# Grouping the value products of a two-pass attention and splitting its causal mask matmuls over the array's row halves

## Chip, cores and metric

The kernel runs on one core of a Trainium2 chip. The metric is device time in microseconds (us) of one execution. TensorE (PE in the rows) runs matmuls, ScalarE (ACT) the exponentials, VectorE (DVE) the row maxima, GpSimd (POOL) masks and small work, and SyncE (SP) issues most transfers.

## What is computed

The reference has two layers, each an attention and a mixture of experts on x (4 x 256 tokens x 128 features) with a context of 4 x 512 tokens x 64 features:

```python
x = x + tanh(g_xattn[0]) * L0_xattn(layernorm(x), ctx)   # 16 heads of 8: causal self-attention plus cross-attention
x = x + tanh(g_ffn[0])   * L0_ffn(layernorm(x))          # 8 experts, top 2, capacity 160
x = x + tanh(g_xattn[1]) * L1_xattn(layernorm(x), ctx)   # one head of 128
x = x + tanh(g_ffn[1])   * L1_ffn(layernorm(x))          # 8 experts, top 2, dense
...
att = einsum('bhqd,bhkd->bhqk', q, k) * scale
att = where(tril, att, -inf)
y   = einsum('bhqk,bhkd->bhqd', softmax(att), v)         # the same again against the context, and added
```

The change lies in the first layer's attention.

## The kernel before

There are 64 pairs of batch and head. Four heads are a quad, so there are 16 quads, numbered 0 to 15; the code's `n` is a quad and `NG` is 16. Two heads that lie in the upper and the lower 64 rows of the array are a pair (`par` 0 and 1). Both passes below work on a pair at once: two matmuls of 64 rows, one for each half of the array, run side by side.

**Pass one** finds the row maxima of the scores. Its units are listed in `pass1`, 96 in all. A "cross" unit is two matmuls of 512 columns (L1410). A "late" unit covers the second 128 queries of two pairs, an "early" unit the first 128 queries of four pairs; both need the causal mask, which is added in PSUM by multiplying an identity with a mask tile (L1402) before the scores are accumulated on it (L1412, L1415). A late unit has 4 mask matmuls and 4 of scores, an early unit 8 and 8. A "turn" unit transposes the maxima (L1387). Each unit fills two of the banks 0 to 3; VectorE reduces it (L1042), and a unit may start when the unit two before it has been reduced (`s1_free`). For every half batch there are 8 cross, 2 late, 1 early and 1 turn.

**Pass two** has 96 steps, six to a quad (k = 0 to 5). `scores2(step)` computes transposed scores of a pair into two banks of a ring of three (banks 4 to 6), and ScalarE takes the exponential of each (L843) into a slot of probabilities. A step of scores therefore has to wait until only one exponential of the step before is left to do:

```python
place = s2_place[2 * step + 1]
if place >= S2_RING:
    pe.wait_ge(p_in, place - S2_RING + 1)
```

`values(n, r)` is round r (0 to 5) of a quad's value products: the four heads write to four groups of 32 columns of the array, with all 128 rows (L1468). Rounds 0 and 1 are the self-attention (256 and 128 columns), 2 to 5 the context (256 columns each). The products of quad n - 1 are issued in the steps of quad n, as `ROUNDS_AT[k]` says. ScalarE takes the finished sums of an earlier quad from bank 7 into `ot_sb` behind the first exponential of a quad (L818), TensorE transposes them in step k = 1 behind the value products (`turn_values`, L1486), and ScalarE takes the result into `o_sb` (L833).

TensorE's order in a step is written out by hand: the pass-one unit that is due, `scores2(step)`, the rounds of `ROUNDS_AT[k]`, at k = 1 `turn_values`, and in steps 81, 83, 89, 91 and 94 work for the output projection and the router (`route_early`). Eighteen units of pass one stand ahead of step 0, then one unit ahead of each step up to step 78. SyncE lays the maxima into `qcat` for the half batch (L550) behind its other loads, and pass two waits for them at steps 0, 12, 24 and so on.

Of the kernel before, what the change touches and what calls it, by code (L numbers as in the profile page):

```python
# [6 lines left out]
BF16 = mybir.dt.bfloat16  # L7
U32 = mybir.dt.uint32
ALU = mybir.AluOpType
# [3 lines left out]
P = 128  # L13
BANK = 512
EPS = 1e-5
CAPACITY_FACTOR = 1.25
NEG = -1.0e30
# [9 lines left out]
def flamingo_gated_kernel(nc, a, out):  # L27
    B, S, D = a["x"].shape
# [15 lines left out]
    PAIR, PAR = H // 2, 2  # L44
# [14 lines left out]
    with ctx:  # L59
        def sb(name, shape, dt=F32):  # L60
            return ctx.enter_context(nc.sbuf_tensor(name, shape, dt))
# [20 lines left out]
        b_col = sb("b_col", [P, 3])  # L82
        b1_col = sb("b1_col", [P, 1])
        bv_col = sb("bv_col", [P, 1])
        bv_wide = sb("bv_wide", [P, D])
        bp_v = sb("bp_v", [P, D])
        b_p = sb("b_p", [P, D])
        b_g = sb("b_g", [P, E])
# [3 lines left out]
        gw_t = sb("gw_t", [P, 2, E])  # L92

        ident = sb("ident", [P, P])
        ident_b = sb("ident_b", [P, P], BF16)
        mask_b = sb("mask_b", [P, P], BF16)
        upto_b = sb("upto_b", [P, P], BF16)
        ones_b = sb("ones_b", [P, KW], BF16)
        iota_e = sb("iota_e", [P, E])
# [56 lines left out]
        def q_place(first, n):  # L156
            return qcat[:, :].rearrange("p a b n -> p (a b n)").bitcast(F32)[:, first:first + n]
# [45 lines left out]
        AFTER_HH = 2 * NF0 * SLOTS  # L203
        eo = q_place(AFTER_HH, 2 * 3 * D).rearrange("p (s t d) -> p s t d", s=2, t=3)
        got = sb("got", [P, 2, NT, D])
        k1_t = q_place(AFTER_HH + 6 * D, NC * P)
        sg = qk_r[:, :, SC:SC + BANK]
        acc = k_place(3, 0, NT * D).rearrange("p (t d) -> p t d", t=NT)
# [13 lines left out]
        def bank(i, n=1):  # L222
            return psum[:, i * BANK:(i + n) * BANK]
# [89 lines left out]
        def linker(eng, s):  # L313

            count = [0]

            def link(ins):
                count[0] += 1
                ins.then_inc(s, 1)
                eng.wait_ge(s, count[0])  # L320
            return link
# [71 lines left out]
        def groups_of(i):  # L393

            return {0: ((0, 2), (2, 4), (4, 8)), 1: ((0, EARLY), (EARLY, 8))}.get(i, ((0, 4), (4, 8)))
# [55 lines left out]
        NG = NHEAD // QUAD  # L451
        STEPS = 3 * QUAD // 2
        TURN_AT = 1
        ROUNDS_AT = ((), (0, 1), (2,), (3,), (4,), (5,))

        TAIL = NG - 5
        assert pass1_before(STEPS * (TAIL + 2)) == len(pass1)
# [136 lines left out]
        def _(pool):  # L594
            link = linker(pool, pool_step)
            made = [0]

            def const(ins):

                made[0] += 1  # L600
                ins.then_inc(consts, 1)
                pool.wait_ge(consts, made[0])
# [3 lines left out]
                                     fill=1.0, base=0, channel_multiplier=1))  # L606
# [4 lines left out]
            def rstd_group(i, first, end):  # L611

                tiles = slice(first, end)
                pool.wait_ge(stats_in[i], end)
                link(pool.tensor_scalar(ln_rstd[:, tiles], ln_mv[:, tiles, 1], EPS, None, ALU.add))
                pool.tensor_tensor(ln_rstd[:, tiles], ln_rstd[:, tiles], half_neg[:, tiles],
                                   ALU.pow).then_inc(rstd_in[i], 1)
# [7 lines left out]
            const(pool.memset(c_t[DC:DC + 1, SC:NC * P], 1.0))  # L625
            for first, end in groups_of(0)[1:]:
                rstd_group(0, first, end)
            const(pool.tensor_copy(ident_b[:, :], ident[:, :]))
            link(pool.memset(mask_b[:, :], 0.0))
            const(pool.affine_select(out=mask_b[:, :], in_=mask_b[:, :], pattern=[[-1, P]], compare_op=ALU.is_ge,  # L630
                                     fill=NEG, base=0, channel_multiplier=1))
            pool.wait_ge(zero_in, 2)
            const(pool.affine_select(out=upto_b[:, :], in_=ones_b[:, 0:P], pattern=[[1, P]], compare_op=ALU.is_ge,
                                     fill=0.0, base=0, channel_multiplier=-1))
# [62 lines left out]
            for head in range(NHEAD):  # L697
                for n in split_before.get(head, ()):
                    split_max(n)
                if head == 5 * QUAD:  # L700
# [5 lines left out]
                                   base=0, channel_multiplier=-1).then_inc(masked, 1)  # L706
# [22 lines left out]
            for e in range(E):  # L729
                pool.wait_ge(dn_taken[0], e + 1)  # L730
                for t in range(NST):
# [3 lines left out]
                                            in_=eo[0:m, e % 2, t, :], in_offset=None, bounds_check=2 * TOK - 1,  # L735
# [586 lines left out]
        def _(pe):  # L1322
# [54 lines left out]
            def pass1_unit(i):  # L1377
                u = pass1[i]
                if i >= 2:
                    pe.wait_ge(s1_free, i - 1)  # L1380
                first = 2 * (i % 2)
                if u[0] == "turn":
                    pe.wait_ge(split_in, u[1] + 1)
                    for t in range(QT):
                        dst = bank(first)[0:2 * PAR * 3 * PP, t * P // 2:(t + 1) * P // 2].bitcast(BF16)
                        src = nmax_p[:, u[1] % 2, PAR * t:PAR * t + PAR].rearrange("p r c q -> p (r c q)")
                        ins = pe.transpose(dst, src, ident_b[:, :])  # L1387
                    ins.then_inc(s1_full, 1)
                    return
                kind, part, t, g = u  # L1390
                b = part // 2
                if kind == "cross" and t == 0 and g == 0:
                    pe.wait_ge(cat_in[b], 16 * 2 * NPROD)
                    pe.wait_ge(pad_in[b], 16 * 4)
                if kind == "late" and part == 0:
                    pe.wait_ge(self_in, 16 * NPROD)
                heads = {"cross": 1, "late": 2, "early": 4}[kind]
                if kind != "cross":
                    for par in range(PAR):
                        dst, w = bank(first + par), BANK // heads  # L1400
                        for n in range(heads):
                            pe.matmul(dst[:, (n + 1) * w - P:(n + 1) * w], ident_b[:, :], mask_b[:, :],  # L1402
                                      start=(n == 0), stop=False, skip_group_check=True)
                for n in range(heads):
                    for par in range(PAR):
                        half = slice(64 * par, 64 * par + 64)
                        q, k = qcat[half, b, heads * g + n], kcat[half, b, heads * g + n]
                        dst = bank(first + par)
                        if kind == "cross":
                            ins = pe.matmul(dst, q[:, S + t * P:S + (t + 1) * P], k[:, S:KW], start=True, stop=True)  # L1410
                        elif kind == "late":
                            ins = pe.matmul(dst[:, n * S:(n + 1) * S], q[:, P:S], k[:, 0:S], start=False, stop=True,  # L1412
                                            skip_group_check=True)
                        else:
                            ins = pe.matmul(dst[:, n * P:(n + 1) * P], q[:, 0:P], k[:, 0:P], start=False, stop=True,  # L1415
                                            skip_group_check=True)
                ins.then_inc(s1_full, 1)
# [25 lines left out]
            def values(n, r, heads=range(QUAD)):  # L1443

                part = 0 if r < 2 else 1 + (r - 2) // 2
                if r == 0:
                    if n <= TAIL:
                        pe.wait_ge(ot_in, n)
                    else:
                        pe.wait_ge(ot_in, n - 1)  # L1450
                    pe.wait_ge(o_clear, 1 + int(n > TAIL))
                    pe.wait_ge(masked, QUAD * n + heads[-1] + 1)
                if n == NG - 1:
                    pe.wait_ge(p_in, s2_place[unit_of(QUAD * n + heads[-1], part)] + 1)
                elif r == 2:
                    pe.wait_ge(p_in, s2_place[3 * QUAD * (n + 1) - 1] + 1)
                for j in heads:
                    head = QUAD * n + j
                    b, h = head // H, head % H
                    p = p_slots[unit_of(head, part) % NPT]  # L1460
                    if r < 2:
                        p = p[:, (0 if r == 0 else S):(S if r == 0 else S + P)]
                        cols, v = slice(r * P, S), QT * b + r
                    else:
                        c = r - 2
                        p = p[:, (c % 2) * S:(c % 2 + 1) * S]
                        cols, v = slice(S, 2 * S), NT + CT * b + c
                    ins = pe.matmul(bank(o_bank(n))[32 * j:32 * j + HA, cols], v_aug[:, v, h, :], p,  # L1468
                                    start=r in (0, 2), stop=r in (1, ROUNDS - 1), skip_group_check=True)
                if r == ROUNDS - 1 and heads[-1] == QUAD - 1:  # L1470
                    ins.then_inc(pv_done, 1)
# [97 lines left out]
            for step in range(STEPS * NG):  # L1569

                n, k = step // STEPS, step % STEPS
# [4 lines left out]
                if n >= 1:  # L1576
                    for r in ROUNDS_AT[k]:
                        values(n - 1, r)
# [176 lines left out]
            for s in range(NHT):  # L1755
                pe.wait_ge([ht_act, ht_dve][s][2], 1)
                pe.matmul(bank(4 + s), w1_q[:, :], h_t[:, s * BANK:(s + 1) * BANK],
                          start=True, stop=True).then_inc(q1_full, 1)
# [61 lines left out]
```

## Time and profile before

| | |
|---|---|
| median of 3 runs | 378.12 us (374.95 to 379.81) |
| the profiled execution | 374.34 us, of which the span from first to last instruction is 372.6 |
| mean granted TensorE clock | 0.948 |
| busy in the span | TensorE 326.8 us, VectorE 233.9, ScalarE 191.7, GpSimd 110.0 |
| first to last step of pass two | 45.7 to 178.4 us |

A time in a row below is in us from the start of the span. Where several instructions are merged in a row, the second number is the time from the start of the first to the end of the last. The end of a matmul is modelled, so the spacing of the starts tells more of TensorE than the durations.

### The profile page before, as it was taken

The numbers are of one execution on the slowest core, as the hardware profiler recorded it, in microseconds if no ns is written. First come the engines' busy times: TensorE is split into PE (matmuls) and PEld (weight loads), VectorE is DVE, ScalarE is ACT, GpSimd is POOL, SyncE is SP. The second block draws the span as 40 slices with busy tenths as digits, with TensorE's granted clock in tenths as the row PEclk, the third lists the DMA queues.
The fourth block names the chain that finished last, engine by engine and source line by source line (L and its number), as shares of the span: only waits on it lengthen the run. The fifth ranks groups of instructions, "written<-read, shape, count | busy, mean of one in ns | idle before, by whom it ended". The sixth has DMA issues, their size and how long they took to land.

```text
span 372.6 us, 7109 instructions
## 1 busy us (share of the span) xinstructions
PE 326.8 (88%) x2696; PEld 188.9 (51%) x2696; DVE 233.9 (63%) x546; ACT 191.7 (51%) x397; POOL 110.0 (30%) x202
## 2 busy tenths in 40 slices
PE   4689799979999999789989799999987599899994
PEld 2446433424434344244476467677755266565662
DVE  5889998858888879466442143332213679649765
ACT  3267388858898888557248323322247143323220
POOL 5526231316433233123575003443350201100000
PEclk9999879989999999899989699999998599989999
DMA  7759792960323005230161560000004000000001
GB/s 177 172 124 210 132 195 56 213 187 4 115 74 102 4 2 173 73 102 3 26 214 35 128 184 10 18 23 21 10 21 118 0 0 3 0 0 2 28 1 28
DMA packets 35777, 27.80 MB, mean 75 GB/s; under 512 B 5579, under 2 KB 33022, under 8 KB 35744
## 3 DMA queue, kind: packets, MB, share of 16 engines
q1 hardware_dynamic: 33574, 25.27, 27.4%
q0 software_dynamic: 1280, 1.88, 1.6%
q8 instruction: 21, 0.34, 0.4%
q10 hardware_dynamic: 890, 0.20, 0.3%
q14 instruction: 12, 0.10, 0.1%
HBM read 11.89 MB, written 5.26 MB: 46 GB/s over the span
## 4 chain that ended last, share of the span: by engine, by line
PE 69%; DVE 13%; ACT 6%; DMA 4%; issue 4%; POOL 2%; ACTq 1%; SPq 0%; POOLq 0%; DVEq 0%
PE psum L1468 12%; PE psum L1672 11%; PE psum L1703 7%; PE psum L1691 4%; DVE nmax L1042 4%; PE psum L1434 4%; PE psum L1650 4%; PE psum L1410 3%; PE psum L1486 3%; PE psum L1402 3%; ACT ot_sb L818 2%; PE psum L1412 1%; PE psum L1655 1%; PE psum L1765 1%; PE psum L1437 1%
## 5 line engine op out<-in xcount | busy, mean ns | idle before, releaser
L1042 DVE TENSOR_REDUCE nmax<-psum 128x2 f32<-128x1024 f32 (+2 forms) x88 | 103.2, 1216 | 15.6 <-PE psum L1410 11.3
L843 ACT ACTIVATE parts<-psum 128x512 f32<-128x512 f32 (+1 forms) x88 | 44.7, 569 | 9.3 <-PE psum L1434 8.8
L1672 PE MATMUL psum<-p_more,kcat 128*128 128x320 f32 x128 | 42.6, 475 | 0.7 <-DVE p_more L1176 0.7
L1185 DVE TENSOR_TENSOR qcat<-psum,qk_r 128x320 f32<-128x320 f32 x32 | 15.7, 491 | 42.8 <-ACT qk_r L886 42.6
L733 POOL DMA_INDIRECT rows_back<-qcat,back_at x24 | 22.9, 953 | 53.1 <-ACT qcat L876 48.2
L886 ACT ACTIVATE qk_r<-psum 128x320 f32<-128x320 f32 x32 | 14.0, 437 | 45.2 <-PE psum L1672 45.2
L1703 PE MATMUL psum<-h_t,kcat 128*128 128x512 f32 x64 | 30.9, 608 | 0.7 <-ACT h_t L854 0.7
L1410 PE MATMUL psum<-kcat,qcat 64*128 64x512 bf16 x128 | 25.9, 404 | 5.5 <-DVE nmax L1042 4.8
L1672 PEld LDWEIGHTS psum<-p_more,kcat 128*128 128x128 f32 x128 | 23.4, 200 | 13.5 <-issue 4.6
L1468 PE MATMUL psum<-parts,v_aug 128*9 128x256 f32 (+1 forms) x352 | 28.9, 373 | 0.0
L1434 PE MATMUL psum<-qcat,kcat 64*128 64x256 bf16 x256 | 25.6, 280 | 3.0 <-ACT p_more L843 1.2
L1468 PE MATMUL psum<-qk,v_aug 128*9 128x256 f32 (+1 forms) x160 | 26.5, 369 | 0.5
L1468 PE MATMUL psum<-qk_r,v_aug 128*9 128x256 f32 (+1 forms) x160 | 26.5, 369 | 0.0
L900 ACT ACTIVATE qk_r<-psum 128x512 f32<-128x512 f32 x16 | 9.6, 597 | 32.6 <-PE psum L1703 32.6
L843 ACT ACTIVATE qk<-psum 128x512 f32<-128x512 f32 (+1 forms) x40 | 20.5, 563 | 10.5 <-PE psum L1439 7.8
L843 ACT ACTIVATE qk_r<-psum 128x512 f32<-128x512 f32 (+1 forms) x40 | 20.3, 551 | 5.6 <-PE psum L1434 3.5
L1691 PEld LDWEIGHTS psum<-kcat,qcat 128*128 128x128 f32 x128 | 17.4, 202 | 9.0 <-issue 5.8
L866 ACT ACTIVATE kcat<-psum 128x512 f32<-128x512 f32 x24 | 14.1, 597 | 12.5 <-PE psum L1599 11.4
L1410 PEld LDWEIGHTS psum<-kcat,qcat 64*128 64x128 bf16 x128 | 6.3, 94 | 26.8 <-DVE nmax L1042 15.0
L1234 DVE TENSOR_TENSOR qcat<-psum,qk_r 128x512 f32<-128x512 f32 x16 | 11.0, 688 | 14.0 <-ACT qk_r L900 8.3
L713 POOL DMA_INDIRECT rows_in<-h_rows,put_at x16 | 16.0, 1000 | 8.5 <-DVE put_at L1153 4.4
L1691 PE MATMUL psum<-kcat,qcat 128*128 128x128 f32 x128 | 18.1, 288 | 0.5 <-DVE qcat L1234 0.5
(225 smaller groups left out, 609.5 us busy)
## 6 DMA issues: line engine op xcount, KB each, us to landing
kcat<-parts SPq DMA_DIRECT2D x18, 192.0 KB, 4.1
qcat<-parts SPq DMA_DIRECT2D x24, 128.0 KB, 3.9
kcat<-ones_b SPq DMA_DIRECT2D x8, 192.0 KB, 5.2
kcat<-in_L_ffn_wi_gate_dram SPq DMA_DIRECT2D x6, 256.0 KB, 3.8
kcat<-in_L_ffn_wi_up_dram SPq DMA_DIRECT2D x6, 256.0 KB, 4.0
kcat<-in_L_ffn_wo_dram SPq DMA_DIRECT2D x6, 256.0 KB, 5.5
parts<-in_L_ffn_w_dram SPq DMA_DIRECT2D x3, 512.0 KB, 5.5
rows_in<-zeros SPq DMA_DIRECT2D x1, 1290.0 KB, 5.8
```

The costliest lines, as they stand in the source:

```text
L713: pool.indirect_dma_start(out=rows_in[0:E * SLOTS, :], out_offset=bass.IndirectOffsetOnAxis(ap=put_at[:, k, t:t + 1], axis=0), in_=h_rows[ ...
L733: pool.indirect_dma_start(out=rows_back[:, :], out_offset=bass.IndirectOffsetOnAxis(ap=back_at[0:m, e, t:t + 1], axis=0), in_=eo[0:m, e % ...
L843: act.activation(p_slots[u % NPT][:, 0:w], s2_bank(s2_place[u])[:, 0:w], ACT.Exp, scale=SCALE).then_inc(p_in, 1)
L1042: dve.tensor_reduce(dst[:, :, n * g:n * (g + 1)], src.rearrange("p (r q k) -> p r q k", r=PAR, q=n), AX.X, ALU.max, negate=True).then_inc( ...
L1185: dve.tensor_tensor(hh[:, e % 2, f, 0:SLOTS], bank(3 + 2 * (i % 2))[:, 0:SLOTS], sg[:, i % 2, 0:SLOTS], ALU.mult).then_inc(hh_in[0], 1)
L1410: ins = pe.matmul(dst, q[:, S + t * P:S + (t + 1) * P], k[:, S:KW], start=True, stop=True)
L1434: ins = pe.matmul(dst[:, c * S:(c + 1) * S], k[:, key:key + P], q[:, S:QW], start=True, stop=True)
L1468: ins = pe.matmul(bank(o_bank(n))[32 * j:32 * j + HA, cols], v_aug[:, v, h, :], p, start=r in (0, 2), stop=r in (1, ROUNDS - 1), skip_grou ...
L1650: pe.matmul(bank(6)[:, t * D:(t + 1) * D], hh[:, e % 2, f, t * P:(t + 1) * P], w_t[e][:, 2, f * P:(f + 1) * P], start=(f == 0), stop=(f == ...
L1672: ins = pe.matmul(bank(2 + 2 * (i % 2) + m)[:, 0:SLOTS], w_t[e][:, m, f * P:(f + 1) * P], xs_t[:, e % 2, :], start=True, stop=True)
L1691: ins = pe.matmul(bank(DN_BANK[n % 4])[:, t * P:(t + 1) * P], hh1[:, n % 2, t * P:(t + 1) * P], w1_t[:, e, 2, :], start=True, stop=True)
L1703: ins = pe.matmul(bank(2 + 2 * (i % 2) + m), w1_t[:, e, m, :], h_t[:, s * BANK:(s + 1) * BANK], start=True, stop=True)
```

## The change

`ROUNDS_AT` puts rounds 0, 1 and 2 of the value products into step k = 1 and rounds 3, 4 and 5 into step k = 3; steps 2, 4 and 5 have none. The mask of a late or early unit is added in two turns, each with matmuls of 64 rows, alternately for the upper and the lower half of the array and for the two banks; a bank's mask takes one matmul from each half of the mask's rows, so there are twice as many mask matmuls (8 in a late unit, 16 in an early one), of the same 128 columns. For the shifted operands the identity and the mask become 256 columns wide, built by GpSimd at the start with one memset more. `bv_wide` becomes a part of `got`.

```diff
-        bv_wide = sb("bv_wide", [P, D])
...
-        ident_b = sb("ident_b", [P, P], BF16)
-        mask_b = sb("mask_b", [P, P], BF16)
+        ident_w = sb("ident_w", [P, 2 * P], BF16)
+        mask_w = sb("mask_w", [P, 2 * P], BF16)
+        ident_b = ident_w[:, P // 2:P // 2 + P]
...
+        bv_wide = got[:, 0, 0, :]
...
-        ROUNDS_AT = ((), (0, 1), (2,), (3,), (4,), (5,))
+        ROUNDS_AT = ((), (0, 1, 2), (), (3, 4, 5), (), ())
...
+            link(pool.memset(ident_w[:, :], 0.0))
             const(pool.tensor_copy(ident_b[:, :], ident[:, :]))
-            link(pool.memset(mask_b[:, :], 0.0))
-            const(pool.affine_select(out=mask_b[:, :], in_=mask_b[:, :], pattern=[[-1, P]], compare_op=ALU.is_ge,
-                                     fill=NEG, base=0, channel_multiplier=1))
+            link(pool.memset(mask_w[:, :], 0.0))
+            const(pool.affine_select(out=mask_w[:, :], in_=mask_w[:, :], pattern=[[-1, 2 * P]],
+                                     compare_op=ALU.is_ge, fill=NEG, base=P // 2, channel_multiplier=1))
...
-                    for par in range(PAR):
-                        dst, w = bank(first + par), BANK // heads
+                    w = BANK // heads
+                    for turn in range(2):
                         for n in range(heads):
-                            pe.matmul(dst[:, (n + 1) * w - P:(n + 1) * w], ident_b[:, :], mask_b[:, :],
-                                      start=(n == 0), stop=False, skip_group_check=True)
+                            for par in range(PAR):
+                                rows = slice(64 * par, 64 * par + 64)
+                                shift = slice(64 * (1 + par - turn), 64 * (1 + par - turn) + P)
+                                pe.matmul(bank(first + par)[:, (n + 1) * w - P:(n + 1) * w], ident_w[rows, shift],
+                                          mask_w[rows, shift], start=(turn == 0 and n == 0), stop=False,
+                                          skip_group_check=True)
```

## Rows read from the trace of the kernel before

**Rows 1.** The page: shares of the chain that ended last.

```profile
PE 69%; DVE 13%; ACT 6%; DMA 4%; issue 4%; POOL 2%; ACTq 1%; SPq 0%; POOLq 0%; DVEq 0%
```

**Rows 2.** The chain in order of time, ScalarE's taking of sums: start, us, what.

```profile
88.29 0.60 ACT ot_sb L818
...
95.58 0.60 ACT ot_sb L818
...
104.08 0.60 ACT ot_sb L818
```

**Rows 3.** Timeline of quad 5, with a turn and cross units only.

```profile
88.44 0.11 PEld L1434 LDWEIGHTS psum<-qcat,kcat 64*128 64x128 bf16 x4 [0.41 <-ACT p_more L843]
...
90.39 0.29 ACT L833 ACTIVATE o_sb<-psum 128x144 f32<-128x144 f32 x1 [0.15 <-PE psum L1486]
90.51 0.11 PEld L1434 LDWEIGHTS psum<-qcat,kcat 64*128 64x128 bf16 x4
...
90.94 1.91 ACT L843 ACTIVATE parts<-psum 128x512 f32<-128x512 f32 x4 [0.25 <-PE psum L1434]
...
93.06 2.17 ACT L843 ACTIVATE parts<-psum 128x512 f32<-128x512 f32 x4 [0.22 <-PE psum L1434]
...
93.51 0.39 PE L1410 MATMUL psum<-kcat,qcat 64*128 64x512 bf16 x2
...
93.74 0.38 PE L1434 MATMUL psum<-qcat,kcat 64*128 64x256 bf16 x4
94.05 0.39 PE L1468 MATMUL psum<-qk,v_aug 128*9 128x256 f32 x1
```

**Rows 4.** Timeline of TensorE in quad 6, which has the masks.

```profile
100.04 0.40 PE L1402 MATMUL psum<-mask_b,ident_b 128*128 128x128 bf16 x4
100.37 0.39 PE L1412 MATMUL psum<-kcat,qcat 64*128 64x256 bf16 x4
100.59 0.38 PE L1434 MATMUL psum<-qcat,kcat 64*128 64x256 bf16 x4
100.91 0.62 PE L1468 MATMUL psum<-parts,v_aug 128*9 128x256 f32 x8
101.46 0.62 PE L1402 MATMUL psum<-mask_b,ident_b 128*128 128x128 bf16 x8
102.01 0.40 PE L1415 MATMUL psum<-kcat,qcat 64*128 64x128 bf16 x8
102.25 0.38 PE L1434 MATMUL psum<-qcat,kcat 64*128 64x256 bf16 x4
```

**Rows 5.** Busy time of the engines in quads 5 and 6, by windows.

```profile
core 0: us, PE busy (x) PEld busy (x) DVE busy (x) ACT busy (x) POOL busy (x), PEclk, DMA share, GB/s
...
88.30:95.60 7.30, 6.78 (x90) 2.63 (x88) 5.91 (x8) 6.67 (x16) 6.20 (x12) 1.00 0.27 104
95.60:104.00 8.40, 8.24 (x116) 3.73 (x114) 7.44 (x8) 6.60 (x15) 2.52 (x7) 1.00 0.11 40
```

**Rows 6.** Waits of TensorE from 54 to 180 us: total, times, longest.

```profile
PE psum L1437 <- DMA qcat<-nmax_t: 2.4, 1, 2.4
PE psum L1387 <- POOL nmax_p L690: 1.8, 1, 1.8
...
PE psum L1506 <- POOL h_rows L668: 0.8, 1, 0.8
```

**Rows 7.** TensorE alone by windows: length, busy, granted clock, DMA share, GB/s.

```profile
40.80:44.20 3.40, 1.55 (x11) 0.95 0.55 100
44.20:47.60 3.40, 2.58 (x14) 0.50 0.50 139
...
156.80:160.20 3.40, 2.47 (x32) 1.00 0.93 273
```

**Rows 8.** Timeline of TensorE in quad 13, at the low clock.

```profile
153.53 0.61 PE L1434 MATMUL psum<-qcat,kcat 64*128 64x256 bf16 x4 [0.58 <-ACT p_more L843]
...
156.52 0.39 PE L1434 MATMUL psum<-qcat,kcat 64*128 64x256 bf16 x4
```

**Rows 9.** Timeline of GpSimd behind its constants.

```profile
25.97 2.61 POOL L654 TENSOR_TENSOR qk_r<-qk,parts 128x1280 f32<-128x1280 f32 x1 [7.75 <-ACT parts L810]
```

## The prediction

> **What bounds the kernel now.** I read the page's chain first: TensorE carries most of it [rows 1]. That average hides that the stretch the change touches has two limits in turn. So next I took the chain in order of time. The taking of sums by ScalarE (L818) is on it once in every quad, and its starts are a ruler: 7.29 us from 88.29 to 95.58, then 8.50 us to 104.08 [rows 2]; eight starts from 88.29 to 142.97 alternate so. Quads with only cross units and a turn take 7.29, quads with three masked units 8.5. The windows say why [rows 5]: in the short quad ScalarE is busy 6.67 of 7.30 us and in the long one 6.60 of 8.40, while TensorE is busy 8.24 of that 8.40. ScalarE's work is the same; it starves longer where TensorE has masks. So a long quad is TensorE's, a short one ScalarE's but for short gaps.
>
> The timeline of the short quad shows the gaps. At the head of a quad TensorE itself waits for an exponential (0.41 before 88.44). Then it issues scores, rounds 0 and 1 and the transposes; the next scores start only at 90.51, and ScalarE idles 0.15 before taking the turned sums and 0.25 before its next exponential at 90.94 [rows 3]. From there four exponentials in 2.17 us, 0.54 each, follow one another. A step then is 1.09 us, two exponentials, and TensorE fits in exactly.
>
> **What one move costs.** A change of shape on the array costs 0.11 us: a round of 256 columns is eight matmuls on four column groups, 0.44 at the spacing of the tail of a group, and the next group starts after 0.55 (100.91 to 101.46); eight full-array masks of 128 columns are 0.44 and the next group starts after 0.55 again (101.46 to 102.01); early scores to pass-two scores, both 64-row shapes, take 0.24 with nothing added (102.01 to 102.25), late ones 0.22 (100.37 to 100.59) [rows 4]. Pass-two scores are 0.22 (0.31 to the values behind them, 93.74 to 94.05), a cross unit 0.23, and from the start of a step's scores to its exponential 0.43 (90.51 to 90.94) [rows 3].
>
> **Grouping the rounds, as a gain.** Before, value products interrupt the 64-row shapes in five steps of a quad, after in two. Three visits less are six changes of shape, 6 x 0.11 = 0.66 us of TensorE time in each of 15 quads. Nothing of the streaming goes away. In a short quad that time isn't on the path at all.
>
> **Grouping the rounds, as a loss.** The ring of three banks sets ScalarE's cover. Scores of a step may start when the first exponential of the step before is done. ScalarE then has three exponentials left to do, 3 x 0.54 = 1.63, and TensorE notices about 0.06 late, so 1.57. Within that TensorE must issue these scores, the rounds, the next pass-one unit, and get the next scores out. Before: 0.22 + 0.11 + 0.44 + 0.11 + 0.22 + 0.43 = 1.53. It fits, by 0.04, which is what the timeline shows. With three rounds in step 3: 0.22 + 0.11 + 3 x 0.43 + 0.11 + 0.22 + 0.43 = 2.38, which is 0.81 beyond the cover. ScalarE starves 0.81 there. In steps 2, 4 and 5 TensorE gets free early, but can't give it back: the same ring stops it, and ScalarE already runs at its own rate. In step 1, where ScalarE starves 0.15 + 0.25 already, round 2 adds its whole 0.43. A short quad so grows by 0.81 + 0.43 = 1.24 us, to 8.5.
>
> **A long quad.** ScalarE's work of 6.6 to 6.9 us is the same as in a short one, and the starving in step 1 as well (0.4 + 0.43). In the path of step 3 a late unit (0.44) takes the place of a cross unit (0.22), so 0.81 + 0.22 = 1.03. The early unit in step 5 fits: 0.22 + 0.68 + 0.43 = 1.33 against 1.57. The short quad's 7.29 + 0.43 + 1.03 is 8.75, and 0.1 more where a cross unit follows the transposes with a change of shape: 8.85, against 8.50. So a long quad turns from TensorE's to ScalarE's and grows by 0.35. Two quads together: +1.6 us.
>
> **The masks.** Each bank's mask now takes two matmuls of 64 rows. Alternating halves run side by side if they do as the early scores do, eight in 0.24; then the streaming stays 0.22 (late) and 0.44 (early), and one or two changes of shape, 0.11 or 0.22, go in each of 24 masked units. Bounds: 0.22 saved in each, or the halves don't overlap and a late mask costs 0.22, an early one 0.44 more. The nearest row, L1415, is the same shape in the same order with different banks, so I take the first [rows 4]. The gain alone would be 0.33 in a long quad, 2 us over six of them; behind the grouped rounds most of it lies where TensorE waits for ScalarE anyway, and it is in the 8.85. The masked units before step 0 stand between full-array projections, so their number of changes stays. If the halves don't overlap, the late unit in step 3's path adds 0.22 per long quad, and the early unit in step 5 makes that path 0.22 + 0.88 + 0.24 + 0.43 = 1.77, 0.20 beyond the cover: 0.42 in each of six quads, 2.5 us in all. GpSimd's extra memset and the doubled widths lie ahead of 7.75 idle us [rows 9]: nothing. `bv_wide` in `got`: nothing, since `got` is filled in the second half of the span.
>
> **Round 2 earlier, other queues.** Round 2 waits for the last exponential of its quad. By the ring that is done before the scores of step 1 start, so nothing new. The sums of a quad are complete two steps earlier; ScalarE's taking, which waits for them, isn't late now. Behind a delayed step stand VectorE's maxima and GpSimd's masks, both with more room than before, and the expert loads on SyncE, which have the whole of pass two as cover.
>
> **The sum.** Quads 1 to 3 would grow by 1.2 + 0.35 + 1.2 = 2.7, but at step 24 TensorE waits 2.4 us for a transfer of the maxima [rows 6] that SyncE issues at the end of an unbroken series of loads which started before step 9. That wait takes the growth up: +0.3. Quads 4 to 11 are four pairs: 4 x 1.6 = +6.4. Quad 12: +0.35, and behind it the wait of 1.8 for GpSimd's split is passed on. Quads 13 to 15 have no pass one. Step 1 costs 0.43, and step 3's path is 2.38 - 0.22 = 2.16 against 1.57, 0.59: together 1.0 in each, +3.0. Against that, round 5 is gone from the end (-0.4), the wait of 0.8 for `h_rows` in step 81 falls where the delay arrives, and the rounds taken from steps 82, 83 and 94 leave projection and router work to start sooner; I take 1.8 for these two together, between the 0.8 of the row and 0.8 + 3 x 0.43. Sum: 0.3 + 6.4 + 0.35 + 3.0 - 0.4 - 1.8 = 7.85, say **+7.9 us**, +2.1%. The rest of the kernel, expert layers and second attention, is shifted and not changed.
>
> The profiled execution took 374.34 us, 1.7 beyond its span of 372.6; it would become 382.2. The median of the runs lies 3.8 above that execution. So the forecast for a median is 378.1 + 7.9 = **386.0 us**.
>
> **Rival A, TensorE alone decides (faster).** If the exponentials were not the limit, the 0.66 of every quad would come off: 15 x 0.66 = 9.9, and 0.1 to 0.2 of 24 masks, about 3: 378.1 - 13 = 365. For it speaks that TensorE is busy 8.24 of 8.40 us in a long quad. Against it: ScalarE's busy 6.67 of 7.30 in a short one, and the 0.04 us that the cover has to spare. It decides from the point at which three rounds together take no more than 0.44 + 0.04 = 0.48 us, against 1.29 by the rows. A mixture of it and the forecast, where ScalarE overlaps more than I think, lands within 2% on the faster side. The Trainium skill, "TensorEngine Tiling (Array Packing)", Key Properties, says that changing the tiling mode drains the engine; the 0.11 us agrees, and by that rule alone the change would come out as this rival. Chance 0.12.
>
> **Rival B, the clock falls too (slower still).** After the change TensorE waits for ScalarE some 2.8 us in a short quad, instead of 0.9, most of it from step 3's end to the next quad's step 1. In the trace the clock went from 2.4 to 1.2 GHz (granted 0.50) behind a stretch in which TensorE was busy 1.55 of 3.40 us; behind one with 2.47 it stayed up [rows 7]. By the same rows' way of counting, a light stretch after the change has six bursts of about 0.39 in 3.6 us, some 2.3 busy, nearer to the second. If it falls, the price per time is in quad 13: 2.99 us from the scores of step 1 to those of step 2 [rows 8], against 2.07 - 0.23 = 1.84 without the turn unit [rows 3], so 1.15. In seven of the quads: +8, 394 us. The Trainium skill, "TensorE: Matmul & The Clock Gate", A second HAM failure mode, tells of matmul groups with short idle pieces between them that make the clock go down and up; no run here has such a stretch yet. Chance 0.17.
>
> **Rival C, something absorbs it (no change).** The k = 3 stall needs every exponential behind it to be late. If more of the delay falls into waits that stand already (2.4, 1.8 and 0.8 us, [rows 6]), +3 remains: 381. For it: these waits are real. Against it: between steps 24 and 72 there is none. Chance 0.11.
>
> **How the numbers follow.** The forecast has 0.60. Two per cent, 7.6 us, is about what a measurement of this kernel tells from no change, and the forecast's +7.9 stands on that bound: half of its 0.60 on either side, since its terms are good to 2 us or so. Slower 0.30 + 0.17 = 0.47, same 0.30 + 0.11 = 0.41, faster 0.12. The range leaves out A, and takes in C, and B up to its seven quads: 378 to 394.
>
> **What would show it.** Right: starts of L818 8.5 and 8.85 us apart; ScalarE idle about 0.8 to 1.0 before the exponential of step 4, once a quad; TensorE waiting for L843 in steps 3 and 5; a round behind a round spaced 0.44; no wait for the transfer at step 24 or a short one; masks with 0.06 from pair to pair, and no 0.11 behind them. Wrong: L818 under 7.3 us apart in short quads (the ring doesn't hold TensorE as I read it), three rounds in less than 1.2 us, masks at 0.11 a pair, or a granted clock under 1 between 90 and 145 us.

## The result, and the profile after

| | before | after |
|---|---|---|
| median | 378.6 us (4 runs, 374.95 to 379.81) | 386.82 us (4 runs, 383.73 to 388.28) |
| ratio | 1 | 1.0232, 95% interval 1.0185 to 1.0279 |
| profiled execution | 374.34 us | 388.28 us |
| busy TensorE, ScalarE | 326.8, 191.7 us | 325.0, 191.2 us |

The change makes the kernel 8.2 us slower at the medians. Slower is clear of the noise; whether it is by more than 2% the interval leaves open. The forecast was 386.0 us, range 378 to 394. Ratios and intervals here and below are estimated from the fast executions alone and need not equal the quotient of the medians beside them. No engine has more to do: busy TensorE time even falls by 1.8 us. The time is in waiting, and the ruler of [rows 2] finds it first. The chain in order of time, after, ScalarE's taking of sums (L820 now):

```profile
89.90 0.60 ACT ot_sb L820
...
98.45 0.60 ACT ot_sb L820
...
107.23 0.60 ACT ot_sb L820
```

The short quad is 8.55 us, forecast 8.5 (7.29 before); the long one 8.78, forecast 8.85 (8.50 before). Two quads have grown by 1.54, forecast 1.6. The windows of these two quads, after:

```profile
core 0: us, PE busy (x) PEld busy (x) DVE busy (x) ACT busy (x) POOL busy (x), PEclk, DMA share, GB/s
90.20:98.80 8.60, 7.08 (x92) 2.83 (x88) 6.34 (x8) 6.69 (x15) 6.16 (x12) 1.00 0.34 127
98.80:107.50 8.70, 7.86 (x132) 4.10 (x130) 7.06 (x8) 6.57 (x15) 2.59 (x8) 1.00 0.01 2
```

Against [rows 5], ScalarE's 6.69 us now stand in 8.60 instead of 7.30, and TensorE is idle more in both. The granted clock is full. The timeline of the short quad, after, shows the two gaps, one in step 1 and one behind step 3:

```profile
90.06 0.39 PE L1440 MATMUL psum<-qcat,kcat 64*128 64x256 bf16 x4
...
92.44 0.29 ACT L835 ACTIVATE o_sb<-psum 128x144 f32<-128x144 f32 x1 [0.58 <-PE psum L1492]
92.56 0.39 PE L1440 MATMUL psum<-qcat,kcat 64*128 64x256 bf16 x4
...
92.98 1.90 ACT L845 ACTIVATE parts<-psum 128x512 f32<-128x512 f32 x4 [0.25 <-PE psum L1440]
...
93.64 0.28 PE L1443 MATMUL psum<-qcat,kcat 64*128 64x256 bf16 x2 [0.47 <-ACT parts L845]
...
93.90 0.39 PE L1474 MATMUL psum<-qk,v_aug 128*9 128x256 f32 x2
...
95.32 0.39 PE L1416 MATMUL psum<-kcat,qcat 64*128 64x512 bf16 x2
95.55 0.38 PE L1440 MATMUL psum<-qcat,kcat 64*128 64x256 bf16 x4
...
95.96 2.17 ACT L845 ACTIVATE parts<-psum 128x512 f32<-128x512 f32 x4 [1.08 <-PE psum L1440]
96.61 0.39 PE L1440 MATMUL psum<-qcat,kcat 64*128 64x256 bf16 x4 [0.47 <-ACT parts L845]
...
97.69 0.28 PE L1443 MATMUL psum<-qcat,kcat 64*128 64x256 bf16 x2 [0.27 <-ACT parts L845]
```

In [rows 3] ScalarE idled 0.15 before the turned sums; now 0.58, which is round 2's 0.43. Behind the three rounds of step 3 (93.90 to 95.32, that is 1.42 = 3 x 0.43 + 0.11 and a little) ScalarE idles 1.08 before its next exponential; in the row of before at the same place, 93.06, it was 0.22. The growth is 0.86, forecast 0.81. Elsewhere TensorE waits for an exponential before the scores of step 3 (0.47 before 93.64), of step 5 (0.47 before 96.61) and of the next quad's step 0 (0.27 before 97.69): it has time to spare and can't use it.

The waits of TensorE between 54 and 200 us, after:

```profile
PE psum L1443 <- ACT parts L845: 5.9, 14, 0.7
PE psum L1440 <- ACT parts L845: 4.0, 8, 0.7
PE psum L1389 <- POOL nmax_p L692: 2.5, 1, 2.5
```

The wait of 2.4 us for the transfer of the maxima [rows 6] is gone, taken up by the delay, as forecast. The wait of 0.8 for `h_rows` is gone too. The one for GpSimd's split is 2.45 instead of 1.84, since without round 5 TensorE comes to it sooner; the step that holds it takes 3.05 instead of 2.98.

### The profile page after: what moved, and what is told of

Same layout as the page of the kernel before. It is cut to its first block, busy times and chain, and to the rows that moved or that the text cites. A ratio compares the mean times of both kernels' runs of the same rounds, so it can differ in the third digit from the quotient of the medians.

```text
span 386.5 us, 7366 instructions
## 1 busy us (share of the span) xinstructions
PE 325.0 (84%) x2824; PEld 194.0 (50%) x2824; DVE 234.1 (61%) x546; ACT 191.2 (49%) x397; POOL 110.7 (29%) x203
## 4 chain that ended last, share of the span: by engine, by line
PE 67%; ACT 11%; DVE 9%; issue 6%; DMA 4%; POOL 2%; ACTq 1%; SPq 0%; POOLq 0%; DVEq 0%
PE psum L1474 12%; PE psum L1678 11%; PE psum L1709 7%; PE psum L1440 5%; PE psum L1656 4%; PE psum L1697 4%; ACT parts L845 3%; DVE nmax L1044 3%; PE psum L1492 2%; PE psum L1605 2%; PE psum L1347 2%; PE psum L1407 2%; ACT ot_sb L820 2%; PE psum L1357 2%; PE psum L1416 2%
## 5 line engine op out<-in xcount | busy, mean ns | idle before, releaser
L1678 PE MATMUL psum<-p_more,kcat 128*128 128x320 f32 x128 | 41.8, 468 | 0.7 <-DVE p_more L1178 0.7
L1440 PE MATMUL psum<-qcat,kcat 64*128 64x256 bf16 x256 | 25.6, 279 | 7.2 <-ACT parts L845 4.0
L1709 PE MATMUL psum<-h_t,kcat 128*128 128x512 f32 x64 | 30.1, 596 | 0.7 <-ACT h_t L856 0.7
L902 ACT ACTIVATE qk_r<-psum 128x512 f32<-128x512 f32 x16 | 9.6, 598 | 30.9 <-PE psum L1709 30.9
L1474 PE MATMUL psum<-parts,v_aug 128*9 128x256 f32 (+1 forms) x352 | 24.3, 365 | 0.0
L1474 PE MATMUL psum<-qk,v_aug 128*9 128x256 f32 (+1 forms) x160 | 23.5, 378 | 0.5
L1474 PE MATMUL psum<-qk_r,v_aug 128*9 128x256 f32 (+1 forms) x160 | 23.5, 378 | 0.0
L1697 PEld LDWEIGHTS psum<-kcat,qcat 128*128 128x128 f32 x128 | 16.3, 191 | 8.4 <-issue 5.3
L1440 PEld LDWEIGHTS psum<-qcat,kcat 64*128 64x128 bf16 x256 | 8.9, 95 | 20.2 <-ACT parts L845 7.1
L1443 PE MATMUL psum<-qcat,kcat 64*128 64x256 bf16 x64 | 9.4, 292 | 9.7 <-ACT parts L845 5.9
```

Source lines behind the costliest of these rows:

```text
L1440: ins = pe.matmul(dst[:, c * S:(c + 1) * S], k[:, key:key + P], q[:, S:QW], start=True, stop=True)
L1678: ins = pe.matmul(bank(2 + 2 * (i % 2) + m)[:, 0:SLOTS], w_t[e][:, m, f * P:(f + 1) * P], xs_t[:, e % 2, :], start=True, stop=True)
L1697: ins = pe.matmul(bank(DN_BANK[n % 4])[:, t * P:(t + 1) * P], hh1[:, n % 2, t * P:(t + 1) * P], w1_t[:, e, 2, :], start=True, stop=True)
L1709: ins = pe.matmul(bank(2 + 2 * (i % 2) + m), w1_t[:, e, m, :], h_t[:, s * BANK:(s + 1) * BANK], start=True, stop=True)
```

## The experiments

The theory: a step's scores may run only one exponential ahead, so between the start of one step's scores and ScalarE's next exponential TensorE has a path, and ScalarE a cover of 1.57 us; what a path has beyond it is lost, and nothing is given back in the light steps. The rivals: TensorE alone decides, so grouping gains (A); the new masks cost; or ScalarE's total work is the only other limit.

The quads are given as the distance of the starts of `ot_sb` on ScalarE, from the steady part of each trace, short and long. Ratios are against the kernel before on the same chip.

**Masks alone.** The changed kernel with the rounds as before:

```diff
-        ROUNDS_AT = ((), (0, 1, 2), (), (3, 4, 5), (), ())
+        ROUNDS_AT = ((), (0, 1), (2,), (3,), (4,), (5,))
```

> The rounds of the value products are spread over the steps as before (0 and 1 in step 1, then one a step); the masks are the new ones, 64 rows each. My theory (the ring of three banks sets what TensorE may take in a step; a change of shape on the array costs 0.11 us): a long quad is TensorE's and loses one change of shape for each of its three masked units, 8.50 down to about 8.2 us; a short quad has no masks and stays at 7.3. In all -1.5 to -2 us, 0.4 to 0.5%. Rival, the halves do not overlap: masks at 0.11 us from pair to pair, long quads 9.3, +5 us. Rival, the masks are where the measured +8 us comes from: about +8.

Measured: 372.22 against 373.73 us, ratio 0.9961 (0.9933 to 0.9990); quads 7.29 and 8.19. The timeline of TensorE in a long quad:

```profile
97.25 0.62 PE L1474 MATMUL psum<-parts,v_aug 128*9 128x256 f32 x8
97.80 0.40 PE L1407 MATMUL psum<-mask_w,ident_w 64*128 64x128 bf16 x8
98.03 0.38 PE L1418 MATMUL psum<-kcat,qcat 64*128 64x256 bf16 x4
...
100.38 0.62 PE L1407 MATMUL psum<-mask_w,ident_w 64*128 64x128 bf16 x16
100.84 0.39 PE L1421 MATMUL psum<-kcat,qcat 64*128 64x128 bf16 x8
```

Eight mask matmuls take 0.23 us to the scores behind them, where four full-array ones took 0.33; sixteen take 0.46, where eight took 0.55 [rows 4]. The halves overlap, and one change of shape, 0.1 us, goes in each masked unit: 3 x 0.1 is the 0.32 of a long quad. The masks gain; they are not where the time went.

**Rounds alone.** The kernel before with the grouping only:

```diff
-        ROUNDS_AT = ((), (0, 1), (2,), (3,), (4,), (5,))
+        ROUNDS_AT = ((), (0, 1, 2), (), (3, 4, 5), (), ())
```

> Only the grouping of the rounds, full-array masks as before. My theory: short quads as with the whole change, 8.55 us; long quads 8.9 to 9.0, since each mask brings its changes of shape into the path of a step; in all +9 to +10 us against before, 1 to 2 more than the whole change. Rival, grouping gains and the new masks lose: a short quad under 7.3 and a time below that of before.

Measured: 382.68 against 373.73 us, ratio 1.0221 (1.0187 to 1.0256); quads 8.55 and 8.90. The short quad is that of the whole change to the hundredth. The long one is 0.12 longer than with the new masks, so behind the grouping little more than a third of the masks' 0.32 is left. In the whole time, +8.3 us by the ratio is under the +9 to +10 expected, and it is not more than that of the whole change (1.0232 and 1.0202).

**One trio at a time.** New masks, and in `ROUNDS_AT` only the first or only the second trio:

```diff
-        ROUNDS_AT = ((), (0, 1, 2), (), (3, 4, 5), (), ())
+        ROUNDS_AT = ((), (0, 1, 2), (), (3,), (4,), (5,))    # first trio
+        ROUNDS_AT = ((), (0, 1), (2,), (3, 4, 5), (), ())    # second trio
```

> New masks; rounds 0, 1, 2 in step 1, and 3, 4, 5 one a step again in steps 3, 4 and 5. My theory: only the term of step 1 is left, 0.43 us for round 2 where ScalarE starves anyway: short quads 7.7, long quads 8.5; about +2.5 us against before. Rival, what costs is each visit with three rounds alike, by its 0.8 us: short quads 8.1, about +6.

> New masks; rounds 0 and 1 in step 1, 2 in step 2, and 3, 4, 5 together in step 3. My theory: the term of step 3, 0.81 us in a short quad: 7.3 + 0.8 to 0.9 = 8.2; long quads 8.7; about +4.5 to +5 us against before. With the run that has the first trio alone the two should add up to the whole change (short quads 7.7 and 8.2 against 8.55, all from 7.3). Rival, the cost comes only from both together (ScalarE's slack is used up once): each alone near 7.4 in a short quad.

Measured: first trio, ratio 1.0107 (1.0073 to 1.0140), quads 7.71 and 8.38; second trio, 1.0096 (1.0062 to 1.0131), quads 8.13 and 8.57. The terms of a short quad are 7.71 - 7.29 = 0.42 (forecast 0.43) and 8.13 - 7.29 = 0.84 (0.81), and they add up: 0.42 + 0.84 = 1.26, and the whole change has 8.55 - 7.29 = 1.26. That each visit with three rounds costs alike, or that the cost comes from both together, is out. The whole-kernel times don't tell the two apart and missed what I expected: +4.0 us for the first trio instead of +2.5, +3.6 for the second instead of +4.5 to +5, by ratios whose intervals overlap. Their quads tell them apart.

**The same with a light ScalarE and VectorE.** Both kernels with half the columns in each exponential of pass two and each maximum of pass one (part of the first attention is left out):

```diff
+            link(pool.memset(p_more[:, :], 1.0))
...
+                w = w // 2
                 act.activation(p_slots[u % NPT][:, 0:w], s2_bank(s2_place[u])[:, 0:w], ACT.Exp,
...
-                                      src.rearrange("p (r q k) -> p r q k", r=PAR, q=n),
+                                      src.rearrange("p (r q k) -> p r q k", r=PAR, q=n)[:, :, :, 0:BANK // n // 2],
```

> The kernel before with less work for the other engines: each exponential of pass two takes the left half of its columns only and each maximum of pass one is taken over the left half of its columns, so the first attention is computed in part; a tile of probabilities is filled with ones at the start. It is the base for its twin with the change. My theory (the ring's round trip from the start of scores to the end of an exponential holds TensorE even when ScalarE has time): short quads 7.0, long quads 8.35 us, both a little under before. Rival, ScalarE's busy share alone is the limit: short quads well under 7, TensorE's own 6.3.

> The changed kernel with the same two cuts (exponentials and maxima over half their columns, so the first attention is computed in part). My theory: short quads 7.6, long quads 8.0, sum 15.6 against 15.4 of its twin, so the loss per two quads falls from 1.5 to about 0.3 us, because a halved exponential shortens ScalarE's part while the steps without rounds are held by the round trip. Rival, ScalarE's busy share alone: with ScalarE light, TensorE is the limit and the grouping pays its 6 x 0.11 us a quad and the masks theirs: 13.7 to 14 for two quads, a gain of 1.5.

Measured: as before, 369.26 us, quads 7.13 and 8.35; as changed, 374.57 us, quads 7.75 and 7.99. Two quads are 15.48 and 15.74: a loss of 0.26, forecast 0.3. The windows of the changed one, a short and a long quad:

```profile
87.70:95.50 7.80, 6.68 (x88) 2.83 (x88) 3.86 (x9) 4.46 (x16) 6.10 (x12) 1.00 0.26 99
95.50:103.50 8.00, 7.41 (x130) 4.09 (x130) 4.15 (x8) 4.42 (x16) 2.72 (x8) 1.00 0.11 41
```

ScalarE is busy 4.46 of 7.80 us and VectorE 3.86. By busy time TensorE alone would be the limit and the grouping should gain 1.5 in two quads. It doesn't: TensorE still waits for exponentials, 1.5 us in these two quads, also ahead of steps without rounds. This row of its timeline is step 0 of the next quad:

```profile
94.89 0.28 PE L1445 MATMUL psum<-qcat,kcat 64*128 64x256 bf16 x2 [0.26 <-ACT parts L847]
```

So the round trip through a ring of three banks, and not only ScalarE's load, keeps TensorE from making up in light steps what it loses in heavy ones. No run has a ring of another size; the ring's part is read from what TensorE waits for. Long quads do gain here, 8.35 to 7.99, but the masks alone bring 0.31 in a long quad, so that this gain is hardly the grouping's. The whole time grows by more than the quads say, 5.3 us at the medians (the first kernel has two runs only). In the profiles pass two grows by 5.45, and 2.9 of it lie in steps 78 to 84, where the clock was at its low level for 6.8 us in the changed one and full in its twin.

**Rounds in pairs.** New masks and rounds in steps 1, 3 and 5:

```diff
-        ROUNDS_AT = ((), (0, 1, 2), (), (3, 4, 5), (), ())
+        ROUNDS_AT = ((), (0, 1), (), (2, 3), (), (4, 5))
```

> New masks; the rounds two by two in steps 1, 3 and 5. My theory: the path of a step with two rounds is 0.22 + 0.11 + 0.86 + 0.11 + 0.22 + 0.43 = 1.95 against a cover of 1.57, 0.38 beyond it, twice a quad: short quads 8.05 to 8.1, long quads 8.35; +3 to +4 us against before, about 1%. Rival, two rounds still fit and only three are too many: short quads 7.3 to 7.4, and a gain by four changes of shape less.

Measured: 378.45 against 376.05 us, ratio 1.0052 (1.0016 to 1.0089); quads 8.13 and 8.35. Two rounds of 256 columns are beyond the cover as well, by (8.13 - 7.29) / 2 = 0.42 each, forecast 0.38. The whole time, +2.0 us by the ratio, is under the +3 to +4 expected, whose low end its interval (+0.6 to +3.3) still holds.

**The changed kernel again.** Unchanged, for what lies outside the quads:

> The changed kernel once more, for what lies outside the quads. In its first profile TensorE, VectorE and ScalarE stood still together at 199 to 206 us with no release that the trace shows, and the clock was low from 15.5 us on. If the change does that, it comes again, and the median is +10 us or more against before; my theory is that it belongs to that execution: here the span grows by what pass two grows, +7.5 to +9 us, with the same 8.55 and 8.77 us quads.

Measured: 384.51 against 376.05 us, ratio 1.0202 (1.0155 to 1.0250); quads 8.55 and 8.77. The growth of the median is what pass two grows. But the two things I had put down to one execution did come again in this profile: TensorE's idle pieces with no release in the trace near 203 us, and the low clock early on. They are taken up below.

**Moving the transposes as well.** The masks alone are faster than both kernels, so one step further along the same account (the edit is against the masks alone):

```diff
-        TURN_AT = 1
-        ROUNDS_AT = ((), (0, 1), (2,), (3,), (4,), (5,))
+        TURN_AT = 3
+        ROUNDS_AT = ((), (0, 1), (2,), (), (3,), (4, 5))
```

> New masks; the transposes of a quad's sums moved from step 1 to step 3, and the rounds as 0 and 1 in step 1, 2 in step 2, none in step 3, 3 in step 4, 4 and 5 in step 5. By the same account of paths and cover: step 1's path loses the transposes, step 3 has them in place of a round, and the pair in step 5 is mostly behind the first wait of the next quad: long quads 8.1, short quads 7.5, together 15.6 like the masks alone (15.5), and 0.9 us less in the last three quads; -2 to -2.5 us against before. Rival, the order of step 1 does not matter for ScalarE: as the masks alone.

> The masks alone once more, beside it on the same chip: long quads 8.19, short quads 7.29, 0.4 to 0.5% faster than before.

Measured: with the transposes moved 374.43 against 374.26 us, ratio 0.9999 (0.9967 to 1.0032), quads 7.44 and 8.11; the masks alone 372.29, ratio 0.9928 (0.9904 to 0.9952), 0.7% where I expected 0.4 to 0.5, quads 7.29 and 8.19. The quads came out as the account says (15.55 for two, against 15.48), the gain of 2 to 2.5 us did not. In its profile pass two is 4.3 us ahead of the kernel before at step 92 and only 1.8 at step 95. Between the two stands one wait that the kernel before doesn't have:

```profile
176.32 0.22 PE L1545 MATMUL psum<-pick_b,upto_b 128*128 128x96 bf16 x1 [2.44 <-DVE pick_b L1115]
```

TensorE's work for the router in step 94 needs `pick_b` from VectorE. VectorE's program takes a quad's transposed sums (172.98) ahead of the router's values (173.74), and with the transposes in step 3 those sums come two steps later, so the values wait behind them. That is a path outside the quads, which the account didn't have. The masks alone stay the best version: 0.9961 and 0.9928 in two sets of runs.

## Why the prediction was right, step by step

**What bounds a quad**, TensorE in long ones and ScalarE in short ones: right. Taking the masks' changes of shape away shortens long quads only (8.19, with 7.29 unchanged).

**The price of a change of shape**, 0.11 us: right, measured 0.09 to 0.10 with the masks. Within a trio a round follows a round after 0.43 us (93.90 to 95.32 above), so the changes between them are gone from TensorE's rows, but no run shows a quad that is shorter for it.

**Step 1, +0.43, and step 3, +0.81**: right, 0.42 and 0.84, each by a run of its own. **The long quad, +0.35**: measured +0.27 (8.77 against 8.50). Its path was sound, my 0.1 for a cross unit behind the transposes was not needed. By the starts of the scores, steps 1 and 3 are 0.43 and 0.77 longer there, and steps 2 and 4, in which TensorE had been late, 0.35 and 0.58 shorter. **The masks' halves overlap**: right, 0.23 and 0.46.

**The sum by stretches.** The starts of the scores of given steps, before and after, give the growth of each stretch: steps 0 to 6, -0.2; 6 to 24, 0.3 (forecast 0.3, the transfer's wait took the rest); 24 to 72, 5.1 (forecast 6.4); 72 to 78, 0.3 (0.35); 78 to 95, 3.0 (1.2). The last products are 0.4 shorter, as forecast, but the last transposes behind them start no sooner: VectorE's copy of the sums starts 0.5 us behind the last product, where it was 0.05. Two terms were off, by -1.3 and +1.8, and nearly cancel: that the total came within 0.3 us of the forecast is partly luck. What made both off is the clock, to which the sum gave nothing:

In quads 4 to 11 the growth of a pair was right (1.54 in the steady part). But before the change the clock was at its low level for 3.4 us right behind the wait at step 24 (TensorE's windows, before: length, busy, granted clock, DMA):

```profile
74.90:78.30 3.40, 1.04 (x14) 0.95 0.90 225
78.30:81.70 3.40, 3.27 (x30) 0.54 0.71 264
```

Quad 4 took 9.49 us there instead of 8.50. After the change the wait and the low clock were gone, so quad 4 shrank by 0.7 instead of growing by 0.3. I had counted the wait and not what the clock did behind it.

In the last three quads the growth is 1.3, 0.65 and 1.1. The opposite happened in the first of them. Both kernels have a low clock behind the wait for GpSimd's split; before, it lasts 3.4 us from 153.1 on, after, 6.8 us from 162 on, in both profiles of the changed kernel. The same windows there, the first row of before and the others of after:

```profile
153.40:156.80 3.40, 3.27 (x28) 0.55 0.31 93
158.80:162.20 3.40, 1.44 (x26) 1.00 0.00 1
162.20:169.00 6.80, 6.12 (x57) 0.50 0.76 228
169.00:172.40 3.40, 2.71 (x24) 0.99 0.06 20
```

Step 81, which lies in it, takes 4.45 us; with the grouping alone it had the full clock and took 2.92, as long as before. That is 1.5 us, and without it these quads come near the forecast. The two things for which I took 1.8 off are in the runs: the wait of 0.8 for `h_rows` is gone, and steps 83 and 89, which have projection and router work and no round any more, are 0.55 shorter each. On the other side the trio of step 3 costs 0.77 in each of the last two quads, where I had 0.59. Whether the change itself makes this low clock longer is open: the masks alone took 10.08 us for steps 78 to 84 with no low clock in one profile, and 12.15 with 6.8 us of it in the other.

Pass two from step 0 to step 95 so takes 141.2 us (47.95 to 189.2) instead of 132.6: +8.6, and +8.5 in the second profile of the changed kernel, against 7.9 + 0.4 forecast for this part, and 8.2 at the medians.

**The profiled execution** grew by 13.9 us, 5.3 more than pass two. Of these, 2.2 lie ahead of step 0 and 3.1 behind step 95. TensorE at the head, before and after:

```profile
0.00:26.00 26.00, 17.12 (x53) 1.00 0.71 157
```

```profile
0.00:26.00 26.00, 17.54 (x43) 0.80 0.70 157
```

The clock was at its low level of 1.2 GHz from 15.5 us on for 10.2 us after the change. (The record of before starts at 20 us and shows full clock from there; its first 20 us are counted as full.) The other profile of the changed kernel and the one with the pairs had the same stretch; the masks alone had none in one profile and 3.4 us of it in the other, which shows that one kernel can have it or not; the grouping alone and the single trios had none, as far as their records go, which start at 19.4 to 21.4 us. The first matmul that the change touches starts at 35.9 us, so I take it for the executions' own, but two of two profiles of the changed kernel don't show that. The first expert's products start 34.2 and 34.3 us behind the start of step 95 in the two profiles of the changed kernel, 31.1 before, 30.9 with the grouping alone, but 34.3 also in the light kernel that has neither edit. That excludes the change as its only cause; what stands behind those idle pieces, marked as issue in the trace, stays open. The grouping's own price doesn't need them: grouping alone has +2.2% and neither of the two in its profile.

**The rivals.** A, TensorE alone decides: fell, even with ScalarE at 4.46 of 7.80 us. For the drain at a change of tiling mode that the Trainium skill names ("TensorEngine Tiling (Array Packing)", Key Properties) the rows show 0.1 us, too small for what was traded for it. B, the clock falls in the light stretches of the quads: fell. A window over the steady quads, after:

```profile
91.00:155.00 64.00, 55.15 (x800) 25.43 (x796) 49.11 (x52) 49.11 (x105) 22.37 (x59) 1.00 0.22 69
```

Granted clock 1.00 throughout, with waits of up to 0.7 us several times a quad; so what "TensorE: Matmul & The Clock Gate" of the Trainium skill tells of short idle pieces (A second HAM failure mode) did not appear here. The longer low clock behind the wait of 2.45 us in quad 13 is the only part of B that came in pass two, some 1.5 us. C, something absorbs it: only the waits of 2.4 and 0.8 us did, which the sum had.

## What to carry to other kernels

Before work is put together on one engine to save changes of its state, add up its longest path between two hand-overs and set it against the work that its neighbour has in hand; a ring of three banks gives 1.57 us here, and an average over the quad would have said that there is room. In a short quad nothing of what a heavy step lost was won back in the light ones, where the ring kept TensorE from running ahead; in a long one only what TensorE had been late was. A longer ring was not tried. A start of one instruction that recurs once per period is a finer ruler than the kernel's time: it told 0.42 from 0.84 us where the medians could not.

## What was not expected

Removing a wait can return more than the wait: the 2.4 us for the transfer at step 24 was followed by 3.4 us at the low clock, and where the delay filled the wait the clock stayed up, so quad 4 came out 0.7 us shorter than before instead of longer. Over all the profiles this holds with one exception: seven have a wait of 1.8 us or more there, and six of them a low clock right behind it; the first trio alone has 2.8 us of wait and none. Of the five others none has it. What the clock gave back there it took again in quad 13. And shrinking each exponential from some 0.54 us to half its columns made the short quad of the kernel before only 0.16 us shorter (7.29 to 7.13), although ScalarE had been busy 6.67 us of it: TensorE is busy 6.83 of the 7.10 us that are left, so near balance the next limit stands right behind.
